# Moving the grid subtraction of an FP4 quantiser from GpSimd to VectorE, with new transfer times in the planner

## What is computed

```python
scale = jnp.maximum(jnp.max(jnp.abs(xb), axis=-1, keepdims=True) / 6.0, 1e-12)   # per block of 16
xn = xb / scale
idx = jnp.searchsorted(_MID, jnp.abs(xn))
q = _GRID[idx] * jnp.sign(xn) * scale        # _GRID = 0, .5, 1, 1.5, 2, 3, 4, 6
...
h = _layernorm(x) * (1 + ca) + sa
x = x + ga * attention(h)
h = _layernorm(x) * (1 + cb) + sb
x = x + gb * down(silu(gate(h)) * up(h))     # gate, up, down: 256x704, 256x704, 704x256, all FP4
```

## Time and profile before

| | |
|---|---|
| median of three runs | 4137.41 us (4131.87 to 4141.31) |
| profiled execution | 4131.86 us, of which the span of the trace is 4129.8 us |
| TensorE busy | 3628.4 us, 88% |
| VectorE busy | 3058.5 us, 74% |
| ScalarE busy | 1912.8 us, 46% |
| GpSimd busy | 1279.1 us, 31% |
| mean granted TensorE clock | 0.951 of full speed |
| first output projection (O of batch 0) | starts at 348.8 us |
| later ones | about every 244.5 us, the last at 3991.6 us |

### The profile page before, as it was taken

One profiled execution on the slowest core, in us unless ns is written; L12 is line 12 of the kernel. 1 busy time (PEld: TensorE's weight loads), 2 busy tenths in 40 slices (PEclk: granted clock), 3 DMA queues, 4 the chain that ended last, 5 costly groups with the idle time before them and its releaser, 6 DMA issues.

```text
span 4129.8 us, 57832 instructions
## 1 busy us (share of the span) xinstructions
PE 3628.4 (88%) x21300; PEld 1919.7 (46%) x21300; DVE 3058.5 (74%) x6061; ACT 1912.8 (46%) x3471; POOL 1279.1 (31%) x918
## 2 busy tenths in 40 slices
PE   1798989989898998989899898998989899898966
PEld 0334444544545445444454445444454444544445
DVE  7577868777786877867687786877777687776835
ACT  2264545544453554545455454544545455454531
POOL 2222324233241423324142332424224142331223
PEclk6799999999999999999999999999999999999987
DMA  2552333323133233313313233332313322332010
GB/s 77 72 71 36 52 58 48 60 39 63 32 63 58 35 56 54 58 40 63 54 31 63 46 56 51 54 55 40 63 36 59 58 41 52 52 48 39 22 26 11
DMA packets 158188, 205.51 MB, mean 50 GB/s; under 512 B 44036, under 2 KB 98004, under 8 KB 157908
## 3 DMA queue, kind: packets, MB, share of 16 engines
q1 hardware_dynamic: 157908, 201.82, 29.2%
HBM read 63.78 MB, written 17.89 MB: 20 GB/s over the span
## 4 chain that ended last, share of the span: by engine, by line
PE 67%; ACT 7%; issue 6%; DVE 6%; DMA 5%; SPq 5%; POOL 4%; POOLq 0%; ACTq 0%; DVEq 0%
PE banks L688 11%; PE banks L708 9%; PE banks L671 8%; PE banks L795 8%; PE banks L772 7%; PE banks L779 7%; ACT arena L861 4%; SPq L543 4%; PE banks L733 4%; DMA sums<-oT 4%; PE banks L753 3%; PE banks L741 3%; PE banks L788 2%; DVE banks L1066 2%; PE banks L674 1%
## 5 line engine op out<-in xcount | busy, mean ns | idle before, releaser
L861 ACT ACTIVATE arena<-banks 128x512 f32<-128x512 f32 (+1 forms) x2432 | 1281.4, 581 | 1300.7 <-PE banks L674 982.1
L1066 DVE CUSTOM_DVE_ANT_0 banks<-banks,mask 128x640 f32<-128x640 f32 (+3 forms) x1024 | 1035.1, 1042 | 121.7 <-PE banks L708 113.2
L671 PE MATMUL banks<-qa,ka 105*128 105x512 bf16 (+3 forms) x3072 | 833.4, 331 | 92.3 <-ACT arena L861 50.9
L708 PE MATMUL banks<-ka,qa 102*128 102x512 bf16 (+3 forms) x3072 | 759.4, 334 | 49.5 <-DVE top L1066 38.1
L688 PE MATMUL banks<-arena,va 128*17 128x512 f32 (+3 forms) x6144 | 648.1, 497 | 20.7 <-ACT arena L861 16.4
L671 PEld LDWEIGHTS banks<-qa,ka 105*128 105x128 bf16 x3072 | 283.4, 98 | 657.1 <-ACT arena L861 346.6
L977 POOL TENSOR_TENSOR hid<-hid,tm 128x704 f32<-128x704 f32 x128 | 215.1, 1680 | 835.2 <-DVE hid L1040 835.2
L708 PEld LDWEIGHTS banks<-ka,qa 102*128 102x128 bf16 x3072 | 261.0, 99 | 387.8 <-DVE top L1066 100.1
L1064 DVE TENSOR_REDUCE top<-banks 128x2 f32<-128x768 f32 (+3 forms) x384 | 384.7, 1041 | 65.7 <-PE banks L713 51.2
L795 PE MATMUL banks<-wdT,hqT 128*128 128x256 f32 x1536 | 373.3, 394 | 2.9 <-ACT hqT L888 2.8
L779 PE MATMUL banks<-wguT,xqT 128*128 128x352 f32 x1024 | 328.7, 464 | 0.0
(11 more groups left out here) (143 smaller groups left out, 4714.4 us busy)
## 6 DMA issues: line engine op xcount, KB each, us to landing
qa<-parts SPq DMA_DIRECT2D x384, 128.0 KB, 4.6
ka<-parts SPq DMA_DIRECT2D x384, 128.0 KB, 5.8
xa<-in_x SPq DMA_DIRECT2D x16, 1024.0 KB, 10.2
xr<-in_x SPq DMA_DIRECT2D x64, 256.0 KB, 2.7
onT<-oT SPq DMA_DIRECT2D x256, 64.0 KB, 4.3
rsumT<-rsum_dram SPq DMA_DIRECT2D x64, 256.0 KB
out_x<-xr SPq DMA_DIRECT2D x64, 256.0 KB, 3.8
ffn_rows<-rows_dram SPq DMA_DIRECT2D x16, 384.0 KB, 4.2
```

The source lines that it names most:

```text
L671: mm = pe.matmul(ps[:, m * w:(m + 1) * w], ka[g][0:KT, h, kt * P:(kt + 1) * P], qa[g][0:KT, h, q0:q0 + w], start=heads < G, stop=heads == ...
L708: mm = pe.matmul(ps[:, at:at + z - a], qa[g][0:KS, h0 + m, qt * P:(qt + 1) * P], ka[g][0:KS, h0 + m, a:z], start=qt > 0, stop=qt == 0 or h ...
L861: nc.scalar.activation(probs[:, s % P_SLOTS, j * heads:(j + 1) * heads, 0:w], ps[:, 0:heads * w].rearrange("p (h q) -> p h q", h=heads), A ...
L1066: nc.vector.tensor_tensor_reduce(out=ps, in0=ps, in1=mask[:, S - w:S], scale=1.0, scalar=MASKED, op0=ALU.add, op1=ALU.max, accum_out=tops) ...
```

## The change

`round_to_grid` now makes four other passes, all on VectorE: scale; one pass with two bit operations that forms the constant (and with 0x40800000, or with 0x0B400000); `max(m, MAGIC) + u`; `max(m, MAGIC) - u`. The result has the opposite sign, and so the block scales are made negative (-1/6, `min`, -1e-12, -BELOW). GpSimd only multiplies by the scale. One `tm` buffer is left, and VectorE no longer waits for GpSimd to be through with the other. In the planner, the costs of the two jobs are set anew and the lags of four transfers are raised: DEN 2.5 to 4.0, NUM 3.0 to 7.0, RDW 2.5 to 6.0, RBC 3.0 to 7.0.

```diff
@@ -274,13 +274,13 @@
 
         old = (b, g - 1) if g else (b - 1, NG - 1)
         done = [("ACT", ("CO", b, g, c)) for c in range(2)]
-        p.add("SP", ("DEN", b, g), 0.7, due, *done, ("DVE", ("RD", *old)), lag=2.5)
-        p.add("SP", ("NUM", b, g), 2.6, due + 1, *done, ("PE", ("O", b - 1, NPAIR - 1)), lag=3.0)
+        p.add("SP", ("DEN", b, g), 0.7, due, *done, ("DVE", ("RD", *old)), lag=4.0)
+        p.add("SP", ("NUM", b, g), 2.6, due + 1, *done, ("PE", ("O", b - 1, NPAIR - 1)), lag=7.0)
         p.add("DVE", ("RD", b, g), 0.4, due, ("SP", ("DEN", b, g)), ("SP", ("RDW", *old)))
-        p.add("SP", ("RDW", b, g), 0.7, due, ("DVE", ("RD", b, g)), ("SP", ("RBC", *old)), lag=2.5)
-        p.add("SP", ("RBC", b, g), 0.7, due, ("SP", ("RDW", b, g)), ("POOL", ("MUL", b, g // 2 - 1) if g >= 2 else ("MUL", b - 1, C - 1)), lag=3.0)
+        p.add("SP", ("RDW", b, g), 0.7, due, ("DVE", ("RD", b, g)), ("SP", ("RBC", *old)), lag=6.0)
+        p.add("SP", ("RBC", b, g), 0.7, due, ("SP", ("RDW", b, g)), ("POOL", ("MUL", b, g // 2 - 1) if g >= 2 else ("MUL", b - 1, C - 1)), lag=7.0)
         if g % 2:
-            p.add("POOL", ("MUL", b, g // 2), 2.2, due + 10.0, *((("SP", (k, b, n)) for n in (g - 1, g) for k in ("NUM", "RBC"))))
+            p.add("POOL", ("MUL", b, g // 2), 2.4, due + 10.0, *((("SP", (k, b, n)) for n in (g - 1, g) for k in ("NUM", "RBC"))))
 
     def residual(b, at):
 
...
@@ -307,8 +307,8 @@
             p.add("DVE", ("LN", b, r), 2.6, due, ("DVE", ("LR", b)), ("SP", ("FROW", b)), ("PE", ("XT", *pair(-2))),
                   ("DVE", ("HQ", *tile(2 * r - 3))))
             p.add("DVE", ("XR", b, r), 1.35, due + 2, ("DVE", ("LN", b, r)), ("DVE", ("XQ", *pair(-1))))
-            p.add("DVE", ("XQ", b, r), 2.75, due + 4, ("DVE", ("XR", b, r)), ring="Q")
-            p.add("POOL", ("XQ", b, r), 2.6, due + 6, ("DVE", ("XQ", b, r)), takes="Q")
+            p.add("DVE", ("XQ", b, r), 2.7, due + 4, ("DVE", ("XR", b, r)), ring="Q")
+            p.add("POOL", ("XQ", b, r), 1.2, due + 6, ("DVE", ("XQ", b, r)), takes="Q")
             pe(("XT", b, r), 0.55, due + 8, ("POOL", ("XQ", b, r)), ("PE", ("UP", *tile(2 * r - 3))),
                ring="A", on="ACT", takes_cost=0.59)
             for t in (2 * r, 2 * r + 1):
...
@@ -321,8 +321,8 @@
                 pe(("UP", b, t), 2.4, late + 2, ("PE", ("GA", b, t, 1)), ("PE", ("UP", *tile(t - 1))), ring="D", on="DVE",
                    takes_cost=0.95, banks=2, then=(("ACT", ("GA", b, t, 1)),))
                 p.add("DVE", ("HR", b, t), 1.75, late + 4, ("DVE", ("UP", b, t)), ("DVE", ("HQ", *tile(t - 1))))
-                p.add("DVE", ("HQ", b, t), 3.15, late + 6, ("DVE", ("HR", b, t)), ring="Q")
-                p.add("POOL", ("HQ", b, t), 3.4, late + 8, ("DVE", ("HQ", b, t)), takes="Q")
+                p.add("DVE", ("HQ", b, t), 3.35, late + 6, ("DVE", ("HR", b, t)), ring="Q")
+                p.add("POOL", ("HQ", b, t), 1.5, late + 8, ("DVE", ("HQ", b, t)), takes="Q")
                 for k in range(2):
                     pe(("HT", b, t, k), 0.55 if k == 0 else 0.3, late + 12, ("POOL", ("HQ", b, t)),
                        ("PE", ("HT", b, t, 0)) if k else None, ("PE", ("DN", *tile(t - 2))), ring="A", on="ACT",
...
@@ -969,13 +969,10 @@
                                                 obg[:, :].unsqueeze(1).broadcast_to((P, 2, D)), ALU.add).then_inc(folded, 1)
                     elif kind in ("XQ", "HQ"):
                         done = in_q[e]
-                        turn = done % 2
                         w = 2 * D if kind == "XQ" else FF
                         u = (xb if kind == "XQ" else hid)[e[2] % 2][:, 0:w]
-                        m, sc = tm[turn][:, 0:w], scales[kind[0]][e[2] % 2][:, :]
+                        sc = scales[kind[0]][e[2] % 2][:, :]
                         pool.wait_ge(rounded, done)
-                        nc.gpsimd.tensor_tensor(u, u, m, ALU.subtract).then_inc(gridded, 1)
-                        pool.wait_ge(gridded, done)
                         blocks = u.rearrange("p (n k) -> p n k", k=BLOCK)
                         nc.gpsimd.tensor_tensor(blocks, blocks, sc.unsqueeze(2).broadcast_to((P, w // BLOCK, BLOCK)),
                                                 ALU.mult).then_inc(quant_done, 1)
...
@@ -1027,24 +1024,24 @@
             def block_scales(src, am, sc, iv):
 
                 step(nc.vector.tensor_reduce(am, blocks(src), AX.X, ALU.max, apply_absolute_value=True))
-                step(nc.vector.scalar_tensor_tensor(out=sc, in0=am, scalar=1.0 / 6.0, in1=tiniest[:, 0:am.shape[-1]],
-                                                    op0=ALU.mult, op1=ALU.max))
+                step(nc.vector.scalar_tensor_tensor(out=sc, in0=am, scalar=-1.0 / 6.0, in1=tiniest[:, 0:am.shape[-1]],
+                                                    op0=ALU.mult, op1=ALU.min))
                 step(nc.vector.reciprocal(iv, sc))
 
             def round_to_grid(u, iv, m):
 
-                step(nc.vector.scalar_tensor_tensor(out=blocks(u), in0=blocks(u), scalar=BELOW, in1=spread(iv),
+
+                step(nc.vector.scalar_tensor_tensor(out=blocks(u), in0=blocks(u), scalar=-BELOW, in1=spread(iv),
                                                     op0=ALU.mult, op1=ALU.mult))
-                step(nc.vector.tensor_scalar(m.bitcast(U32), u.bitcast(U32), 0x7F800000, None, ALU.bitwise_and))
-                step(nc.vector.tensor_scalar(m, m, 1.0, MAGIC, ALU.max, ALU.mult))
-                return nc.vector.tensor_tensor(u, u, m, ALU.add)
+                step(nc.vector.tensor_scalar(m.bitcast(U32), u.bitcast(U32), 0x40800000, 0x0B400000, ALU.bitwise_and, ALU.bitwise_or))
+                step(nc.vector.scalar_tensor_tensor(out=u, in0=m, scalar=MAGIC, in1=u, op0=ALU.max, op1=ALU.add))
+                return nc.vector.scalar_tensor_tensor(out=u, in0=m, scalar=MAGIC, in1=u, op0=ALU.max, op1=ALU.subtract)
 
             def quantise(tile, n):
                 nb = n // BLOCK
-                m, am, sc, iv = tm[0][:, 0:n], amax["H"][:, 0:nb], scales["H"][0][:, 0:nb], inv["H"][:, 0:nb]
+                m, am, sc, iv = tm[:, 0:n], amax["H"][:, 0:nb], scales["H"][0][:, 0:nb], inv["H"][:, 0:nb]
                 block_scales(tile, am, sc, iv)
                 step(round_to_grid(tile, iv, m))
-                step(nc.vector.tensor_tensor(tile, tile, m, ALU.subtract))
                 return nc.vector.tensor_tensor(blocks(tile), blocks(tile), spread(sc), ALU.mult)
 
             def run():
...
@@ -1148,9 +1145,7 @@
                     elif kind in ("XQ", "HQ"):
                         done = in_q[e]
                         u, w = (xb[e[2] % 2][:, :], 2 * D) if kind == "XQ" else (hid[e[2] % 2][:, 0:FF], FF)
-                        if done > 2:
-                            dve.wait_ge(quant_done, done - 2)
-                        round_to_grid(u, inv[kind[0]][:, :], tm[done % 2][:, 0:w]).then_inc(rounded, 1)
+                        round_to_grid(u, inv[kind[0]][:, :], tm[:, 0:w]).then_inc(rounded, 1)
                     elif kind == "UP":
                         t = e[2]
                         dve.wait_ge(a_free, in_a["GA", b, t, 1])
...
@@ -1180,7 +1175,7 @@
             step(nc.vector.memset(slope_row[:, 7, 1:6:2], 1.0))
             dve.sem_inc(tiny_set, 1)
             nc.vector.memset(va[:, :, :, HD:VW], 1.0)
-            nc.vector.memset(tiniest[:, :], 1e-12)
+            nc.vector.memset(tiniest[:, :], -1e-12)
 
             dve.wait_ge(pool_set, 4)
             dve.wait_ge(slope_in, 48)
```

4 lines of the change are left out of this document (2 added, 2 removed).

## The result

The changed kernel takes 4254.6 us, the median of four runs (4251.6 to 4257.5). The kernel before took 4134.6 us beside it (4130.6 to 4141.3). The ratio is 1.0284, with a 95% interval from 1.0268 to 1.0300: **120 us slower**. The prediction said 4134 us, between 4065 and 4195. The time lies outside the range, on the side that had 4 chances in 10.

What follows compares the result with a forecast made beforehand. TensorE was busy 88% of the span, so time could be won only where it is idle or slow. Terms +23 - 41 + 13 + 10 - 8 = -3 us gave a median near 4134 us, range 4065 to 4195.

Steps and rivals of the forecast that it cites:

- Term 1: Output projection O: MUL 5.8 us later, 3.9 us of wait filled by attention jobs; +23 us, bounds -28 and +65.
- The first rival: At O, MUL comes in time and every batch gains 3.9 us: -59 instead of +23, 4052 us; chance 0.1.
- Term 2: VectorE's waits at RD, groups 1 and 2: added row maxima shrink TensorE's gaps; -41 us, bounds 0 and -87.
- a fuller clock: TensorE's half clock at group 1 in 12 batches: half of 12 x 1.7 us regained, -10 us.
- Term 3: More quantiser work on VectorE: net +39 us, a third passed on as +13 us, bounds 0 and +39.
- relief of contention, 25 us: VectorE beside GpSimd: contention put at 100 us, a quarter relieved by GpSimd's smaller work, 25 us.
- Term 4: T jobs waiting for ScalarE in the new order: a fifth more than 50.9 us, +10 us, bounds 0 and +60.
- Term 5: Last batch and start: shorter quantiser path -7, RDW behind XIN +2, weight tiles -3; sum -8 us.
- as was said of RDW: Last batch: RDW now stands behind XIN, costing +2 us.
- attention runs dry: Behind O, TensorE and ScalarE take turns: 4 us a batch, +60 instead of +10, 4184 us; chance 0.28.

Runs made afterwards that it cites:

- the old order: Changed kernel with all planner numbers of the kernel before, so only the quantiser is new: 4133.3 us, ratio 0.9999 to the kernel before.
- The run with MUL first: Changed kernel with MUL of groups 2 and 3 moved on GpSimd ahead of FOLD and OB, in all batches but the first: 4176.1 us.

## Why the prediction was wrong

**Term 1, the projection (+23).** Right. MUL starts 12.3 us after the broadcast (12.4 forecast), FOLD at 10.2, and batch 4 waits 9.86 us (10.3 forecast). In all the wait grew by 18 us. What the term's sum did not bring out is what it had in hand: the three S ahead of O fill time only if MUL isn't held back, and MUL ahead of FOLD was worth 78 us here. The first rival had that mechanism, at 82 us.

**Term 2, the waits at RD (-41).** The mechanism is right, and alone it gives 34 us. In the changed kernel VectorE waits 66 us at RD, against 144 before, and still no gain shows. TensorE's gaps behind RD of groups 1 and 2 are gone, but one wait took their place directly. In the changed kernel LN's row, the RD behind it and TensorE's transposes stand like this (VectorE, then TensorE):

```profile
1432.58 3.76 DVE L1135 SCALAR_TENSOR_TENSOR xb<-xb,rs,ffn_rows 128x256 f32<-128x256 f32 x2
1436.37 0.35 DVE L1087 RECIPROCAL rsums<-sums 128x32 f32<-128x32 f32 x1
```

```profile
1437.83 0.87 PE L788 MATMUL banks<-ident,hid 128*128 128x128 f32 x6 [2.49 <-DVE top L1063]
```

There is now a gap at group 0, where before there was none, and it halves the clock as the one at group 1 did. Stretches of 2 us, the clock third from the end:

```profile
1437.00:1439.00 2.00, 1.17 (x15) 0.80 (x16) 2.00 (x5) 0.48 (x1) 0.00 (x0) 1.00 1.11 137
1439.00:1441.00 2.00, 2.00 (x12) 1.61 (x9) 2.00 (x5) 1.15 (x4) 0.00 (x0) 0.52 1.07 121
1441.00:1443.00 2.00, 2.00 (x8) 1.63 (x7) 1.86 (x6) 0.30 (x1) 0.00 (x0) 0.62 0.25 20
```

The 10 us that the term took for a fuller clock did not come either: by parts of the table above, the mean granted clock of the second fell from 1.00 to 0.98, and the third's went from 0.98 to 0.97.

**Term 3, VectorE's work (+13).** Alone it costs nothing measurable. VectorE's +52 us in the old order is near the +39; the bit pass took 539 ns in the mean, and the two passes behind it 938 and 1074, against 1038 for the one add before. But "relief of contention, 25 us" is a number that belongs to an order. In the new one the contention grew: VectorE is busy 149 us longer. I had read a mean excess of 0.15 us as rare collisions. It is made of a few meetings that repeat in every batch, and in the new order LN, which the term did not look at, meets GpSimd in three of its four pairs, where before it was mainly in one.

**Term 4, the new order elsewhere (+10, bounds 0 and +60).** **This step failed.** The order costs 121 us with the new quantiser. 27 of them are the projection's (its wait is 134.0 us in the old order, 161.4 in the new), which leaves 94, and what the waits at RD gave back is already taken off. The run with MUL first says nearly the same: it is 43 us above the old order although its projection waits 46 us less, 89 in all. Against that stands a forecast of 10. I sized the term as a fifth of one row of waits, the T that wait for ScalarE. Those rows grew by 55 us (53.6 to 108.5), the waits for the read-outs of hid by 34, and TensorE's own busy time by 43, of which the quantiser alone brings 12 in the old order. What share each of them has in the 94 us is not separated, since waits on other rows became shorter. The trace of before could price what was moved away from a wait. It could not price waits that did not exist yet, and with nine numbers of the planner changed there were many places for them. The upper bound should have been open.

**Term 5, the ends (-8).** Right, in size too: the first projection starts 3.2 us earlier, and from the start of the last one to the end it is 130.7 us and not 138.2, together -10.7. The wait of the earlier trace rows is 4.76 us where 4.8 was forecast; the last projection's wait grew from 17.3 to 19.0, as was said of RDW.

```profile
4184.01 1.51 PE L788 MATMUL banks<-ident,hid 128*128 128x128 f32 x6 [4.76 <-POOL hid L977]
```

**The rivals.** The second, attention runs dry, came nearest. Its price of 4 us a batch in waits for ScalarE is what came (55 us in 15 batches). Its place was wrong: none of it is directly behind O, and most stands in the parts between the second transpose and the next projection. It was one of three losses. The other two, the new gap behind RD of group 0 with its slow clock and the waits for read-outs, were in no rival.

## What to carry to other kernels

When a change puts new numbers into a planner as well as new code on the chip, run the two apart before anything else: here the code cost nothing and the order 121 us, 93 of them by costs of which GpSimd's were truer than the ones they replaced. Look at an engine's busy share part by part of the loop. An engine busy 76% of a batch was busy 85% of the part that grew most, and the part grew by as much as the engine's work in it. The busy time of a part has to be taken as that of the whole batch is: adding up rows that overlap makes it 4 to 5 us too long here. And try a single move by itself: RD moved by hand, the new quantiser and the old order gave 4100 us, with the split in halves 4092 (0.9892 of before, 0.9877 to 0.9907), while the whole set of new numbers gave 4255.

## What the runs showed of the hardware

A VectorE pair of instructions with two SBUF inputs took 3.77 us beside GpSimd's split and 0.88 us alone. Halving GpSimd's two-input instructions cut it to 2.56 us, and replacing them by one-input scalings to 2.31 us. Moving it away brought it back to 0.88 us and passed half of what LN gained (25 of 49 us) to the quantiser's two-input passes, which I had not expected; VectorE's busy time in all stayed as long.
